# Two layers of attention and experts: score products parted by a value product, an earlier front of layer 1, and block ends without GpSimd's drain

## What is computed

```python
x = x + L0_xattn(layernorm(x), ctx, ctx)     # 8 heads of 4 features, output projection, biases
x = x + L0_ffn(layernorm(x))                 # 8 experts, 2 per row, at most 640 rows an expert, SiLU gate, 1024 wide
x = x + L1_xattn(layernorm(x), ctx)          # 16 heads of 16 features
x = x + L1_ffn(layernorm(x))                 # 15 experts, 3 per row, GELU gate, and a shared expert of 512
# attention: scores = q . k * scale; softmax over the 512 keys of the sequence; out = softmax . v
```

## Time and profile before

| | us |
|---|---|
| median of 3 runs | 1383.97 |
| lowest and highest | 1379.62, 1384.95 |
| the profiled execution's own time | 1380.14 |
| its span | 1378.4 |
| TensorE busy | 1183.1 (86%) |
| VectorE busy | 737.0 (53%) |
| ScalarE busy | 536.8 (39%) |
| GpSimd busy | 406.3 (29%) |
| mean granted TensorE clock, share of full | 0.877 |

### The profile page before, as it was taken

One profiled execution on the slowest core, in us unless ns is written; L12 is line 12 of the kernel. 1 busy time (PEld: TensorE's weight loads), 2 busy tenths in 40 slices (PEclk: granted clock), 3 DMA queues, 4 the chain that ended last, 5 costly groups with the idle time before them and its releaser, 6 DMA issues. The chain is left out here.

```text
span 1378.4 us, 20546 instructions
## 1 busy us (share of the span) xinstructions
PE 1183.1 (86%) x6794; PEld 771.7 (56%) x6795; DVE 737.0 (53%) x1374; ACT 536.8 (39%) x1096; POOL 406.3 (29%) x443
## 2 busy tenths in 40 slices
PE   4799988279999999998458888889996999999987
PEld 1323334179999999998213334344444755555544
DVE  5567533245665556543356665656625634444447
ACT  2176443043454345432505454455561422322310
POOL 4122354522343224300501112120001146666520
PEclk9688555579999999999658999889997899999999
DMA  3410200142144213300542243221105452222243
GB/s 104 184 47 1 77 29 13 36 144 74 62 131 131 78 55 126 112 20 20 171 133 88 84 129 90 89 70 48 40 1 185 174 206 75 76 76 83 68 139 113
DMA packets 82559, 123.44 MB, mean 90 GB/s; under 512 B 17618, under 2 KB 54953, under 8 KB 82226
## 3 DMA queue, kind: packets, MB, share of 16 engines
q1 hardware_dynamic: 72018, 94.92, 21.3%
q0 software_dynamic: 10464, 27.52, 6.3%
HBM read 89.06 MB, written 35.39 MB: 90 GB/s over the span
## 5 line engine op out<-in xcount | busy, mean ns | idle before, releaser
L1779 DVE TENSOR_REDUCE M<-S 128x2 f32<-128x1024 f32 x128 | 153.8, 1220 | 51.2 <-PE S L1390 39.2
L1675 ACT ACTIVATE PT<-S 128x512 f32<-128x512 f32 x256 | 138.9, 594 | 93.9 <-PE S L1414 85.1
L222 POOL TENSOR_TENSOR w12l<-stage,w12h 128x1024 fp32r<-128x1024 f32 x28 | 67.8, 2421 | 199.8 <-ACT w12h L216 199.8
L2055 PE MATMUL pg<-W,hold 128*128 x248 | 121.0, 610 | 2.9 <-ACT hold L2137 1.2
L1198 DVE TENSOR_TENSOR HTm0l<-HFm,HTm0h 128x320 fp32r<-128x320 f32 x128 | 122.0, 953 | 1.0
L1204 DVE TENSOR_TENSOR HFm<-Um,SGm 128x320 f32<-128x320 f32 x128 | 62.3, 487 | 79.5 <-ACT SGm L1167 79.1
L1167 ACT ACTIVATE SGm<-Gm 128x320 f32<-128x320 f32 x128 | 56.0, 438 | 118.0 <-PE Um L1125 117.2
L910 DVE TENSOR_REDUCE M<-S 128x2 f32<-128x1024 f32 x64 | 77.1, 1222 | 34.0 <-PE S L426 30.1
L1138 PE MATMUL Ym<-w3h,HTm0h 128*128 128x256 f32 x320 | 93.3, 292 | 0.0
L1390 PE MATMUL S<-KS,QS 48*128 48x512 f32 x256 | 71.2, 554 | 25.6 <-issue 9.5
L1427 PE MATMUL PV<-PT,VA 128*32 128x256 f32 x1024 | 87.1, 416 | 5.1 <-issue 3.0
(11 more groups left out here) (273 smaller groups left out, 2502.2 us busy)
## 6 DMA issues: line engine op xcount, KB each, us to landing
stage<-in_W12T SPq DMA_DIRECT2D x32, 512.0 KB
stage<-in_W3T SPq DMA_DIRECT2D x16, 512.0 KB
W<-in_fc1T SPq DMA_DIRECT2D x2, 3840.0 KB, 24.5
KS<-scrk SPq DMA_DIRECT2D x96, 64.0 KB, 2.2
QS<-scrq SPq DMA_DIRECT2D x96, 64.0 KB, 2.2
W<-yk SPq DMA_DIRECT2D x16, 384.0 KB, 7.9
xs<-zeros POOLq DMA_DIRECT2D x10, 512.0 KB, 4.5
XSm<-xs SPq DMA_DIRECT2D x8, 640.0 KB, 4.9
```

The costliest lines, as they stand in the source:

```text
L222: pool.tensor_tensor(ew.part(1, s, c), ew.stage[:, c % STAGES, :], ew.part(0, s, c).bitcast(F32), ALU.subtract).then_inc(ew.low_done, 1)
L1675: act.activation(PT[:, at % SLICES, 2 * hp + j, :], S2[:, j, :], ACT.Exp, scale=HP ** -0.5).then_inc(exp_done, 1)
L1779: dve.tensor_reduce(M[:, n % 3, at:at + 2 * TPB + 1:2 * TPB], out[:, :, :], AX.X, ALU.max).then_inc(S1.done(("max", c)), 1)
L2055: m = pe.matmul(H[:, c % 2, :], XST[:, c % 2, k, :], W1[:, k, bass.ds(e, 1), :], start=(k == 0), stop=(k == KD - 1))
```

## The change

Four things are changed, and nothing that is computed:

- In both attention stages `scores(s)` becomes `scores(s, j)`. The product j = 0 stays where it was, the product j = 1 comes behind the half value product, ahead of `turn_out` and the side tasks.
- In the front of `layer1` the keys of group 1 are loaded at t = -6 instead of -2, and the queries of group 0 at t = -2 instead of -1, between the stores of units 2 and 3.
- VectorE's `keep_v(0)` comes behind `apply(0, 0)` at t = -5.
- All five blocks are opened with `no_gpsimd_drain=True`: GpSimd doesn't drain at their ends, and the engines meet by semaphores alone.

```diff
-        block = ctx.enter_context(nc.Block())
+        block = ctx.enter_context(nc.Block(no_gpsimd_drain=True))
...
-            def scores(s):
+            def scores(s, j):
 
                 n, i = divmod(s, BEATS1)
                 kt, hp = pairs(i)
-                if i == 0:
+                if i == 0 and j == 0:
                     pe.wait_ge(nm_loaded[n % 2], 16 * SHIFT * (n // 2 + 1))
-                for j in range(2):
-                    at = slice(64 * j, 64 * j + 64)
-                    wait(pe, exp_done, 2 * s + j - 1)
-                    pe.matmul(S2[:, j, :], KS[at, n % SLOTS1, hp, kt * P:(kt + 1) * P], QS[at, n % SLOTS1, hp, :],
-                              start=True, stop=True).then_inc(s2_ready, 1)
+                at = slice(64 * j, 64 * j + 64)
+                wait(pe, exp_done, 2 * s + j - 1)
+                pe.matmul(S2[:, j, :], KS[at, n % SLOTS1, hp, kt * P:(kt + 1) * P], QS[at, n % SLOTS1, hp, :],
+                          start=True, stop=True).then_inc(s2_ready, 1)
...
                 if 0 <= s < NC1:
-                    scores(s)
+                    scores(s, 0)
                 if s >= 3 and (s - 3) // 2 < TPB * NG1:
                     values(*divmod((s - 3) // 2, TPB), (s - 3) % 2)
+                if 0 <= s < NC1:
+                    scores(s, 1)
                 if s >= 13 and (s - 13) % BEATS1 == 0 and (s - 13) // BEATS1 < NG1:
                     turn_out((s - 13) // BEATS1)
...
                 for n in range(NG1):
-                    if t == max(8 * n - 10, -6):
+                    if t == (max(8 * n - 10, -6) if n != 1 else -6):
                         load_stack("k", n)
-                    if t == (max(8 * n - 9, -1)):
+                    if t == max(8 * n - 9, -2):
                         load_stack("q", n)
...
                 if t == -5:
                     apply(0, 0)
+                    keep_v(0)
...
-                    if name == "v":
+                    if name == "v" and b:
                         keep_v(b)
...
-    with nc.Block() as block:
+    with nc.Block(no_gpsimd_drain=True) as block:
```

More of the change, by code:

```diff
@@ L438, in turn_max @@
                 pe.transpose(MISC[0:2 * GH * TPB, 0:P], MS[:, n % 2, :], env.ident[:, :]).then_inc(misc_ready, 1)
-            def scores(s):
+            def scores(s, j):
                 n, i = divmod(s, BEATS0)
                 kt, h = units(i)
-                if i == 0:
+                if i == 0 and j == 0:
                     pe.wait_ge(nm_loaded[n % 2], 16 * SHIFT * (n // 2 + 1))
-                for j in range(2):
-                    wait(pe, exp_done, 2 * s + j - 1)
-                    pe.matmul(S2[:, j, :], KS[rows(h + j), n % 4, kt * P:(kt + 1) * P], QS[rows(h + j), n % 4, :],
-                              start=True, stop=True).then_inc(s2_ready, 1)
+                wait(pe, exp_done, 2 * s + j - 1)
+                pe.matmul(S2[:, j, :], KS[rows(h + j), n % 4, kt * P:(kt + 1) * P], QS[rows(h + j), n % 4, :],
+                          start=True, stop=True).then_inc(s2_ready, 1)
             def values(n, kt, part):
```

1 line of the change is left out of this document (added).

## The result

| | us |
|---|---|
| changed kernel, median of 4 runs | 1435.30 (1427.63 to 1437.74) |
| kernel before, median of 4 runs beside it | 1382.65 (1379.62 to 1384.95) |
| ratio | 1.0373, 95% interval 1.0327 to 1.0418 |
| profiled execution of the changed kernel, its span | 1437.74, 1436.0 |

The change makes the kernel 52 us slower; no change (1383) was forecast, in a range that ended at 1397. In the two profiled executions the spans differ by 57.6 us. By the stages' first loads that is: layer 0 +32.9, experts +0.4, layer 1 +26.3 (its front -4.1, the rest +30.4), the last stage -2.0. The layers' values here end with SyncE's first load of the stage behind them (277.62 and 1050.57 before, 310.53 and 1110.15 after).

The account below looks back on a forecast made before the run. TensorE's work or waits in a beat were taken to set most of the attention stages' cost. Terms -3.5 - 3.3 + 0.5 + 6.7 = +0.4 us gave 1383; the likeliest case's range was 1377 to 1390, the whole range 1366 to 1397.

Parts of the forecast that it names:

- 26 beats of layer 0 "at full clock" and 23 at half: Layer 0's 49 beats with maxima and scores, an added slot at 0.33 or 0.54 each: 21.0 us more TensorE time.
- The prediction's last sentence: Wrong if layer 0's beats don't grow, waits come back on another line, or layer 0's clock changes.
- The rival on the clock: Layer 0: a denser TensorE gets 2.4 GHz, -17 us against the forecast, 1367; chance 0.07.
- Block end of layer 0, -3.5: End of layer 0: without GpSimd's drain SyncE issues the experts' first load at about 274.1, -3.5 us.
- The other three ends at 0: Ends of experts0, layer 1 and ffn1: drains hidden by VectorE's and SyncE's last work, 0 us.
- Front, -3.3: Layer 1's front: query loads and first maxima begin 3.3 us earlier; bounds -1.8 and -3.6.
- Layer 1's parting, +0.5: Layer 1's beats: 17 us of waits gone against 17.5 us of added slots, net +0.5; bounds -20 and +17.5.
- 17 us of waits: Layer 1: part of the 20.0 us in 53 waits for exponentials that parting would take away.
- Layer 0's parting, +6.7: Layer 0's beats: 21.0 and 2.0 us added, 12.3 of waits and 4.0 hidden slots taken off; bounds -16.4 and +23.
- where I had 2.0: Layer 0's 15 end beats without maxima: only side tasks add slots, about 2.0 us.
- the 12.3 us of the sum: Layer 0: three quarters of 16.4 us in 40 score waits for the exponentials, taken as gone.
- The slower rival: Layer 0: the wait moves behind a later exponential instead of going; layer 0 +19.0, in all +13, 1397; chance 0.18.

Follow-up runs that it names:

- e4: Kernel before with only the block ends changed (no GpSimd drain); 0.9982 of the kernel before, 1380.94 us.
- e9: Changed kernel with neither layer parted (front, keep_v(0) and block ends kept), repeated as a reference; 0.9961 of the kernel before, 1378.38 us.
- e15: Changed kernel with layer 0 unparted and layer 1 parted only in plain beats from 93 to 118; 1.0011 of the kernel before, 1385.14 us.
- e1: Changed kernel with layer 0's two score products together again, layer 1 parted; 1.0112 of the kernel before, 1400.22 us.
- e5: Changed kernel with layer 1 unparted and layer 0's two score products both behind the value half, not parted; 1.0235 of the kernel before.
- e10: Changed kernel with layer 1 unparted and layer 0 parted from beat 26 on only; 1.0185 of the kernel before.
- e11: Changed kernel with layer 1 unparted and layer 0 parted only in beats 18 to 22; 1.0019 of the kernel before, 1382.91 us.
- e6: Changed kernel with layer 1 unparted, layer 0 parted, and the maxima's first product issued twice from beat 15 on; 1.0268 of the kernel before.
- e13: Changed kernel with layer 0 unparted and layer 1's two score products both behind the value half, as a pair; 1.0124 of the kernel before.
- e14: Changed kernel with layer 0 unparted and layer 1 parted only in the six beats 120 to 125; 0.9887 of the kernel before.
- e12: Changed kernel with layer 0 unparted and layer 1 parted up to beat 117 only; 1.0086 of the kernel before, 1394.71 us.
- e8: Changed kernel with layer 0 unparted and layer 1 parted only in the 57 beats that aren't plain; 1.0047 of the kernel before.
- e7: Changed kernel with layer 0 unparted and layer 1 parted only in its 71 plain beats; 1.0244 of the kernel before.

## Why the prediction was wrong

**The step that failed is the one that is not in the sum: every beat was costed at the clock it had before.** I counted 26 beats of layer 0 "at full clock" and 23 at half and multiplied slots by 0.33 and 0.54. The slot of 0.41 at half clock was even less than I took. But adding it changed which beats had the full clock: 22 went from 2.4 to 1.2 GHz, +25.7 us with their slots, of which some 17 are the clock by the estimate above. The prediction's last sentence names a change of layer 0's clock as a sign of being wrong, and that sign came. The rival on the clock had only the direction up, from "a denser TensorE". By its own reasoning (four products in one slot were what was dense) it should have had the other sign: the change spreads the same products over 1.97 us instead of 1.56.

- *Block end of layer 0, -3.5*: right, 3.5. The other three ends at 0: nothing in the stages behind contradicts it; e4's -2.3 is all of them together.
- *Front, -3.3*: about right, -4.1, and e9 has -4.5. The split was off. Adds, copy and store were 2.9, 1.9 and 1.9 us sooner where I had 3.4, 2.2 and 2.2; the landing took 3.4 (718.70 to 722.07) for my 3.1. The rest came from the query loads of group 0 standing alone: the first maxima start 4.6 us behind the first of them, 6.0 before.
- *Layer 1's parting, +0.5*: of the right size for beats at full clock: +4.6 in 88 of them, 0.0 in beats 93 to 119. The waits left the plain beats and the slots appeared where I put them (`turn_max` beats 2.41 instead of 2.16, beats with side tasks 0.2 to 0.4 more). The premise that 17 us of waits could be taken away by themselves was wrong, as e15 shows: they came back in the next beat. This term too was priced at the clock of the old trace: parting layer 1 cost 24 us by medians. In the trace of the changed kernel 23.5 us lie from beat 121 on, most of them at half clock where it was full before; in e1's trace that part is 10.8.
- *Layer 0's parting, +6.7*: 33.6 measured. In beats at half clock in both +4.8, in the part without maxima +5.5 where I had 2.0; the 25.7 of the beats that lost the clock come on top. Waits did go, but fewer than the 12.3 us of the sum: 20 of those 28 beats have scores, and 20 slots of 0.41 are 8.2, of which 4.8 showed.
- *The slower rival*, the wait that moves, had +13 in layer 0 by ScalarE. The waits did move in the list of waits, but behind the value product: the beat at half clock has the length of its slots, 1.97, and no wait in it.

**What stays open.** In layer 0 it is shown that the order with two slots keeps 1.2 GHz after a fall (e5, e10, e11). Why that order keeps it was only argued; e6, made to show it, did not. In layer 1 it is shown that the loss needs no lone products (e13) and doesn't come from the beats at the last fall alone (e14), and that with the old order at the end the tail is as before while 16.3 us remain (e12). Which of the parted beats ahead make a fall last longer is not known. In e11 and e15, with these beats in the old order, it lasted 20 and 17 us instead of 7, so how soon the clock returns there is a near thing in the old order as well.

**The better version.** The front and the block ends without any parting beat both kernels, by about half a per cent against the kernel before: 0.9940 (0.9915 to 0.9964) and, run again, 0.9961 (0.9929 to 0.9993). e14, which adds six parted beats, had 0.9887, but its interval overlaps theirs.

## What to carry to other kernels

When the granted clock moves between 1.2 and 2.4 GHz within a stage, don't price a new order at the clock of the old trace: mark the beats where the clock falls, and ask what the order does in the beats that follow each fall, since a slot of 0.4 us can decide over 80 us at half clock. A wait that the list shows is worth its length only if the starts beside it are further apart than in a beat without it, and the next beat doesn't wait instead; try it in one beat before counting it in fifty. And products on different row groups that start together are a slot that a new order can lose, so look at which group the next product needs.

## What was not expected of the hardware

- TensorE busy for 40.68 of 41.46 us stood at 1.2 GHz throughout, and in the same beats with one slot less at 2.4 GHz (22.78 of 23.71 us).
- The falls came at the same beats whatever the order: at about 46, 57, 79, 89 and 121 of layer 1 in every trace. What differed was how long they lasted: 7 to 68 us for the one at 121. Two more, at about 36 and 68, stood in every trace but those of e5 to e8. On that chip beats 32 to 40 took 17.1 us in e5 against 22.8 in e9, and beats 64 to 72 17.1 against 22.3: where the stall was short, the clock didn't fall.
- A second product in succession on a row group, beside others, cost 0.14 us a beat at 1.2 GHz though a slot was free for it (e6).
- The same kernel took 1359.3 us on one chip and 1381.9 to 1383.9 in the other sets, 1.7 to 1.8% apart, more than most of the differences tested here. The traces of the old order differ in a few stalls: besides those two, beats 52 to 56 of layer 0 took 9.4 us in e7 and 19.4 in e12. Why is not known.
